# First attention: post weights applied to evicted outputs, and the inverse and the eviction ordered ahead of the next maximum and exponent

## The reference, cut to what matters

```python
logits = jnp.einsum('bhid,bhjd->bhij', q, k) * SCALE        # 4 batches, 16 heads of 8, 1024 tokens
logits = jnp.einsum('bhij,gh->bgij', logits, Wpre)          # heads mixed before the softmax
attn = jax.nn.softmax(logits, axis=-1)
attn = jnp.einsum('bhij,gh->bgij', attn, Wpost)             # heads mixed after it
out = jnp.einsum('bhij,bhjd->bhid', attn, v)
out = out.transpose(0, 2, 1, 3).reshape(b, n, DIM)
return out @ Wout.T + bout
```

## Time and profile before

| what | value |
|---|---|
| time, median of 3 runs | 2481.05 us (2480.69 to 2481.33) |
| time of the profiled execution | 2480.47 us |
| its span in the profile | 2478.7 us |
| busy in the span: PE, DVE, ACT, POOL | 89%, 84%, 74%, 50% |
| first attention in the profile | about 72 to 1506 us |
| feed-forward, second attention, feed-forward | the rest, to 2478.7 us |

### The profile page before, as it was taken

How to read it: one execution, slowest core, us unless ns; L and a number is a source line. 1 busy time by engine, 2 the same in 40 slices (tenths; PEclk the granted TensorE clock), 3 DMA queues, 4 the chain that set the end, 5 groups by cost and what they waited for, 6 DMA issues and landing times. The chain is left out here.

```text
span 2478.7 us, 62316 instructions
## 1 busy us (share of the span) xinstructions
PE 2199.3 (89%) x22576; PEld 1502.2 (61%) x22576; DVE 2077.6 (84%) x3160; ACT 1822.4 (74%) x2674; POOL 1237.8 (50%) x1482
## 2 busy tenths in 40 slices
PE   5899999999999999999999994556899999999556
PEld 3466676666766676666766664443455555555544
DVE  6899999999999999999999995655799999997473
ACT  1788888888888888888888882115799998998002
POOL 3445444444444544445444452300788888887030
PEclk9999999999999999999999997669799999999866
DMA  2799999999999999999999993006222222222001
GB/s 93 121 196 187 196 187 192 191 192 189 194 189 194 184 197 192 190 189 192 192 189 191 192 194 71 1 8 207 70 69 72 70 69 70 70 69 51 29 1 34
DMA packets 1183691, 333.54 MB, mean 135 GB/s; under 512 B 1145968, under 2 KB 1174512, under 8 KB 1183216
## 3 DMA queue, kind: packets, MB, share of 16 engines
q1 hardware_dynamic: 1182320, 326.97, 74.2%
q10 hardware_dynamic: 1152, 3.62, 0.4%
HBM read 30.57 MB, written 14.68 MB: 18 GB/s over the span
## 5 line engine op out<-in xcount | busy, mean ns | idle before, releaser
L329 PE MATMUL a_out_ps<-a_vs,a_pT 128*128 128x129 f16 x4096 | 726.0, 221 | 48.4 <-ACT a_own_out L378 46.6
L416 DVE SCALAR_TENSOR_TENSOR a_parts<-a_probs,a_parts 128x1024 f16<-128x1024 f32 x512 | 653.2, 1276 | 115.1 <-ACT a_parts L369 115.1
L333 PE MATMUL a_out_ps<-a_vs,a_pT 128*128 128x129 f16 x4096 | 724.5, 219 | 0.0
L331 PE MATMUL a_out_ps<-a_vs,a_pT 128*128 128x128 f16 x4096 | 724.4, 218 | 0.0
L361 ACT ACTIVATE a_probs<-a_score_ps,a_negmax 128x1024 f32<-128x1024 f32 x512 | 571.8, 1117 | 164.9 <-DVE a_negmax L410 164.8
L410 DVE TENSOR_REDUCE a_negmax<-a_score_ps 128x1 f32<-128x1024 f32 x512 | 621.2, 1213 | 2.4 <-PE a_score_ps L315 2.4
L369 ACT ACTIVATE a_parts<-a_probs 128x1024 f16<-128x1024 f32 x512 | 543.5, 1061 | 0.6 <-DMA a_pT<-a_parts 0.6
L329 PEld LDWEIGHTS a_out_ps<-a_vs,a_pT 128*128 128x128 f16 x4096 | 396.4, 97 | 146.1 <-ACT a_own_out L378 99.1
L331 PEld LDWEIGHTS a_out_ps<-a_vs,a_pT 128*128 128x128 f16 x4096 | 402.9, 98 | 44.6
L477 POOL TENSOR_TENSOR acc<-acc,a_own_out 128x256 f32<-128x256 f32 x256 | 247.9, 969 | 352.3 <-DVE a_parts L416 346.4
L311 PE MATMUL a_score_ps<-kh,a_qs 128*128 128x512 f16 x1024 | 388.6, 379 | 10.3 <-DVE a_qs L401 7.0
(11 more groups left out here) (199 smaller groups left out, 2701.4 us busy)
## 6 DMA issues: line engine op xcount, KB each, us to landing
a_pT<-a_parts SPq DMA_TRANSPOSE x512, 5.0
b_qs<-q_parts SPq DMA_DIRECT2D x128, 64.0 KB, 2.0
b_ks<-k_parts SPq DMA_DIRECT2D x128, 64.0 KB, 1.9
q_parts<-b_parts SPq DMA_DIRECT2D x32, 128.0 KB, 1.9
k_parts<-b_parts SPq DMA_DIRECT2D x32, 128.0 KB, 1.9
v_parts<-b_v_all SPq DMA_DIRECT2D x4, 1024.0 KB, 4.6
b_vs<-v_parts SPq DMA_DIRECT2D x32, 128.0 KB, 2.1
b_sent_pT<-b_sent_parts SPq DMA_TRANSPOSE x256, 2.3
```

Of the source, the lines that this page charges most:

```text
L329: pe.matmul(out[:, 0:D + 1], hi, vs[:, G % 2, 0, j, 0:D + 1], start=j == 0, stop=False, skip_group_check=True)
L331: pe.matmul(out[:, 0:D], hi, vs[:, G % 2, 1, j, 0:D], start=False, stop=False, skip_group_check=True)
L333: last = pe.matmul(out[:, 0:D + 1], lo, vs[:, G % 2, 0, j, 0:D + 1], start=False, stop=j == JB - 1, skip_group_check=True)
L416: dve.scalar_tensor_tensor(out=parts[:, T % RING_P, 1, :], in0=probs[:, T % RING_P, :], scalar=PSCALE, in1=parts[:, T % RING_P, 0, :], op0 ...
```

## The change

Two things change in `attend_a`.

- **Post weights.** The values are no longer scaled for each group. They are split into their 16-bit parts once a batch: `vs` has a slot for each of the four batches, the first is made ahead of the loop, the others while the batch before is worked on (steps 24, 26 and 28 of its 128). The post weights are applied to the evicted outputs by a new POOL operation `weigh(pair)` from `own_out` into `weighed`, and `add` reads `weighed`. POOL runs `weigh` of one pair and then `add` of the pair before it, and at the end one more `add`. The eviction now waits for `weigh` of the pair before last (semaphore `weighed_ready`), not for its `add`.
- **Order.** In step i of DVE the inverse now stands ahead of the maximum of tile i, in step i of ACT the eviction ahead of the exponent of tile i.

```diff
             for i in range(TILES_A + AH + 2):
+                if i >= AH + 2 and i % 2 == 0:
+                    evict((i - AH - 2) // 2)
                 if i < TILES_A:
                     exponentiate(i)
-                if i >= AH + 2 and i % 2 == 0:
-                    evict((i - AH - 2) // 2)
...
             for i in range(TILES_A + AH + 2):
+                if i >= AH + 2 and i % 2 == 0:
+                    invert((i - AH - 2) // 2)
                 if i < TILES_A:
                     row_max(i)
-                if i >= AH + 2 and i % 2 == 0:
-                    invert((i - AH - 2) // 2)
...
                 act.wait_ge(rden_ready, pair + 1)
                 if pair >= 2:
-                    act.wait_ge(added, pair - 1)
+                    act.wait_ge(weighed_ready, pair - 1)
...
-                G, t = T // TPB, T % TPB
-                if t == 0:
-                    pe.wait_ge(vlo_made, G + 1)
+                b = T // (HA * TPB)
+                if T % (HA * TPB) == 0:
+                    pe.wait_ge(vlo_made, b + 1)
...
+            def weigh(pair):
+
+                pool.wait_ge(evicted, 2 * pair + 2)
+                if pair >= 2:
+                    pool.wait_ge(added, pair - 1)
+                g = 2 * pair // TPB % HA
+                w = wpost[:, g * D:(g + 1) * D][:, None, :].broadcast_to([P, 2, D])
+                slot = 2 * pair % 4
+                pool.tensor_tensor(weighed[:, pair % 2, :, :], own_out[:, slot:slot + 2, :], w,
+                                   ALU.mult).then_inc(weighed_ready, 1)
...
             pool.memset(vs[:, :, 0, :, D:], 1.0).then_inc(ones_ready, 1)
+            high_v(0)
+            low_v(0, 0)
+            low_v(0, 1)
             pool.memset(acc[:], 0.0).then_inc(cleared, 1)
             pool.wait_ge(cleared, 1)
-            for i in range(TILES_A + AH + 4):
-                G, t = i // TPB, i % TPB
-                if i < TILES_A and t < 5:
+            for i in range(TILES_A + AH + 2):
+                b, step = i // (HA * TPB) + 1, i % (HA * TPB) - 3 * TPB
+                if b < NB and step in (0, 2, 4):
                     pace(i)
-                    if t in (0, 1):
-                        scale_v(G, t)
-                    elif t == 2:
-                        high_v(G)
+                    if step == 0:
+                        high_v(b)
                     else:
-                        low_v(G, t - 3)
-                if i >= AH + 4 and i % 2 == 1:
+                        low_v(b, step // 2 - 1)
+                if i >= AH + 3 and i % 2 == 1:
+                    pair = (i - AH - 3) // 2
                     pace(i)
-                    add((i - AH - 4) // 2)
+                    weigh(pair)
+                    if pair >= 1:
+                        add(pair - 1)
+            add(TILES_A // 2 - 1)
```

More of the change, by code:

```diff
@@ L265, in attend_a @@
         own_out = st.sb(s, "a_own_out", [P, 4, D])
+        weighed = st.sb(s, "a_weighed", [P, 2, 2, D])
         qs = st.sb(s, "a_qs", [P, 2, 2, SEQ], F16)
[L267 to L268 removed]
+        vs = st.sb(s, "a_vs", [P, NB, 2, JB, D + 2], F16)
         score_ps = [st.ps(s, f"a_score_ps{i}", [P, SEQ]) for i in range(3)]
@@ L328, in times_v @@
                     hi, lo = pT[:, T % RING_T, 0, j, :], pT[:, T % RING_T, 1, j, :]
-                    pe.matmul(out[:, 0:D + 1], hi, vs[:, G % 2, 0, j, 0:D + 1], start=j == 0, stop=False,
+                    pe.matmul(out[:, 0:D + 1], hi, vs[:, b, 0, j, 0:D + 1], start=j == 0, stop=False,
                               skip_group_check=True)
-                    pe.matmul(out[:, 0:D], hi, vs[:, G % 2, 1, j, 0:D], start=False, stop=False,
+                    pe.matmul(out[:, 0:D], hi, vs[:, b, 1, j, 0:D], start=False, stop=False,
                               skip_group_check=True)
-                    last = pe.matmul(out[:, 0:D + 1], lo, vs[:, G % 2, 0, j, 0:D + 1], start=False,
+                    last = pe.matmul(out[:, 0:D + 1], lo, vs[:, b, 0, j, 0:D + 1], start=False,
                                      stop=j == JB - 1, skip_group_check=True)
@@ L444, in pace @@
                     pool.wait_ge(lo_ready, min(i - 1, TILES_A))
-            def scale_v(G, c):
-                if c == 0 and G >= 1:
-                    pool.wait_ge(vlo_made, G)
-                own = slice(c * JB // 2, (c + 1) * JB // 2)
-                src = v[:, (G // HA) * SEQ + c * HALF:(G // HA) * SEQ + (c + 1) * HALF]
-                w = wpost[:, (G % HA) * D:(G % HA + 1) * D][:, None, :].broadcast_to([P, JB // 2, D])
-                pool.tensor_tensor(vtmp[:, own, :], src.rearrange("p (j d) -> p j d", j=JB // 2), w,
-                                   ALU.mult).then_inc(v_scaled, 1)
@@ L456, in high_v @@
-            def high_v(G):
-                pool.wait_ge(v_scaled, 2 * G + 2)
-                if G >= 2:
-                    pool.wait_ge(pv_done, TPB * (G - 1))
-                pool.tensor_scalar(vs[:, G % 2, 0, :, 0:D], vtmp[:], 1.0, 1.0, ALU.mult, ALU.mult).then_inc(vhi_made, 1)
-            def low_v(G, c):
-                pool.wait_ge(vhi_made, G + 1)
-                own = slice(c * JB // 2, (c + 1) * JB // 2)
-                last = pool.tensor_tensor(vs[:, G % 2, 1, own, 0:D], vtmp[:, own, :], vs[:, G % 2, 0, own, 0:D],
-                                          ALU.subtract)
+            def high_v(b):
+                pool.tensor_scalar(vs[:, b, 0, :, 0:D], v[:, b * SEQ:(b + 1) * SEQ].rearrange("p (j d) -> p j d", j=JB),
+                                   1.0, 1.0, ALU.mult, ALU.mult).then_inc(vhi_made, 1)
@@ L469, in low_v @@
+            def low_v(b, c):
+                pool.wait_ge(vhi_made, b + 1)
+                own = slice(c * JB // 2, (c + 1) * JB // 2)
+                src = v[:, b * SEQ + c * HALF:b * SEQ + (c + 1) * HALF]
+                last = pool.tensor_tensor(vs[:, b, 1, own, 0:D], src.rearrange("p (j d) -> p j d", j=JB // 2),
+                                          vs[:, b, 0, own, 0:D], ALU.subtract)
                 if c == 1:
                     last.then_inc(vlo_made, 1)
+            def weigh(pair):
[7 more added lines that the diff above has]
+                                   ALU.mult).then_inc(weighed_ready, 1)
@@ L472, in add @@
             def add(pair):
-                pool.wait_ge(evicted, 2 * pair + 2)
+                pool.wait_ge(weighed_ready, pair + 1)
                 at = (2 * pair // TPB // HA) * TPB + 2 * pair % TPB
-                slot = 2 * pair % 4
-                pool.tensor_tensor(acc[:, at:at + 2, :], acc[:, at:at + 2, :], own_out[:, slot:slot + 2, :],
+                pool.tensor_tensor(acc[:, at:at + 2, :], acc[:, at:at + 2, :], weighed[:, pair % 2, :, :],
                                    ALU.add).then_inc(added, 1)
```

4 lines of the change are left out of this document (1 added, 3 removed).

## The result

The changed kernel takes 2459.04 us (2456.97 to 2459.72) against 2481.16 us: a ratio of 0.991, 95% interval 0.9893 to 0.9927, so 22 us won where 57 were forecast. Its profiled execution took 2459.72 us with a span of 2457.9 us.

A forecast was written before the change was run, and what follows sets the result against it. DVE and ACT were taken to set the pace while PE waits 0.87 us a group. Gains of 53.9 (62 groups), 1.3 and 3.5 less 1.9 give 56.8 us: 2424 us, range 2418 to 2450.

The forecast's parts named there:

- What bounds the kernel now: First attention: a DVE-ACT loop, 5.00 us for two tiles, makes the eviction late; PE loses 0.87 us a group of 22.15.
- The eviction leaves the path and fits into ACT's wait; DVE's inverse costs nothing: New order: loop falls from 5.00 to 4.51 us; eviction of 0.49 to 0.62 us fits ACT's 0.63 us wait; inverse free.
- POOL's wait of 0.4 us is inside the 0.87: Eviction's wait for POOL's `add`, 0.4 us on the loop's third pair, goes; already counted in PE's 0.87 us a group.
- Low part behind `weigh` and `add`, up to 0.33 us: DVE's low part overlaps POOL's two operations by at most 0.33 us, taken as lost four times a group: 1.3 us.
- The start: POOL's new work at the very start may hold the first `low_q`: 0 to 1.1 us lost, 0.5 taken.
- The end: After the last eviction POOL does more, +1.4 us; DVE is no longer late, 3.5 us less.
- The pace after it: DVE 19.75, ACT 18.8, loop 19.2 to 20.3 us a group, all under PE's 21.28, so PE takes over; 0.87 won.
- The prediction's own signs of being wrong: Low parts of 1.6 us or more; L369 waiting for `a_pT`; PE stalled at L311; turns above 2.66 us at clock 1.00.
- Another pace than PE's takes hold: Rival: DVE or transpose landings set the pace, only part of the gain, 2453 or 2456 us; chance 0.15.
- It does nothing: Rival: PE's stall is a late transpose, or the transpose queue takes no more than one in 2.77 us; 2481 us, chance 0.04.

The follow-up runs named there:

- e10: Changed kernel with two stages ahead of 64 transposes each, free of engine waits, the second beside 3200 PE matmuls; 2810.05 us with both stages.
- e7: Changed kernel with 32 more long-fulfilled waits in each POOL step, packed into 16 more instructions; 2470.82 us, ratio 0.9952 to the kernel before.
- e6: Changed kernel with the high part's two products in one 256-column matmul, 44 instead of 60 PE instructions a tile; 2431.76 us, ratio 0.9796.
- e5: Changed kernel with two transposes a tile, the high part's sent as soon as it is made; 2573.69 us, ratio 1.0373 to the kernel before.
- e12: Changed kernel with one 128x4096 transpose for two tiles and eight instead of four slots for the parts; 2427.58 us, ratio 0.9789.
- e3: Changed kernel with five instead of four slots for the parts; 2460.62 us, ratio 0.9916 to the kernel before.
- e4: Changed kernel with only the high part transposed and read twice by the product, half the transposed data; 2423.65 us, ratio 0.9764.
- e11: Changed kernel with the old order of inverse and eviction, weights on the outputs, only the high part transposed; 2454.07 us, ratio 0.9893.
- e1: Kernel before with the new order of inverse and eviction alone, post weights still folded into the values; 2548.94 us, ratio 1.0271.
- e9: Kernel before with the new order alone and eight instead of four slots for the evicted outputs; 2459.29 us, ratio 0.9910.

## Why the prediction was wrong

**The queue's time adds up.** With 2.473 us a transpose, 0.86 us a 16 KB fetch (both e10) and 0.17 us an 8 KB one (e7, the least certain of the three), the queue is taken, out of 1200 us, for:

| kernel | transposes | q8 | q14 | us taken |
|---|---|---|---|---|
| before | 434 | 102 | 46 | 1169 |
| after | 443 | 105 | 44 | 1193 |
| e6 | 451 | 79 | 46 | 1191 |
| e7 | 439 | 104 | 98 | 1192 |
| PE's pace, after's fetches | 451 | 105 | 44 | 1213 |

Before, the queue was 97% full with DVE and ACT setting the pace; the change moves it to 99.4%, and there it stops. PE's pace would need 1213 us of every 1200. For e7 this isn't a test of its own, since its count gave the 0.17. Halves in e5 come to (1200 - 97 x 0.86 - 45 x 0.17) / 817 = 1.36 us each, so a whole, which is 2.47, saves 0.24 us over two halves. A pair in one transpose would by that be 4.70 us, with the fetches 2.57 us a tile, under 2.66; e12 bears out that it is under 2.66. (The expectation had 4.47 us, with the fetches not yet taken out of the halves.)

The packet records give a count that needs none of these prices: the time, out of the same 1200 us, in which no packet of a transpose is under way. It is 33 us before, 12 after, 15 in e3, 9 in e6, 16 in e7 and 1 in e5, against 499 in e4. So by this count too the queue is 97% full before the change and 99% after it. In e12 it is 31 us at PE's pace: (1200 - 31) / 451 = 2.59 us a tile, fetches included, is about what the paired transposes need.

**By the prediction's steps.** *What bounds the kernel now*: right; the loop of DVE and ACT gave way, and where the queue has room (e4) exactly 2.66 us comes out. *The eviction leaves the path and fits into ACT's wait; DVE's inverse costs nothing*: right by e4 and e11, 30 us. *POOL's wait of 0.4 us is inside the 0.87*: right, since 0.48 is left of the stall in e11, but its weight was underrated. In the new order that wait would have grown to 229 us (e1). So the weights' move is what lets the order pay, or else more slots (e9). *Low part behind `weigh` and `add`, up to 0.33 us*: 1.45 instead of 1.21 us, thus 0.24, in two of four pairs (at 688.26 and 700.18 us). The overlap was 0.37 us, a little over the 0.33 of the working, and it cost nothing in e4. The Trainium skill ("SBUF — State Buffer", section "Who interferes with whom") has the overlap go to whoever started first, and this low part began 0.37 us before the `add` at 687.90 ended:

```profile
687.90 0.73 POOL L476 TENSOR_TENSOR acc<-acc,a_weighed 128x256 f32<-128x256 f32 x1
```

The trace agrees on who yields: the `add` kept its 0.73 us, and the low part lost 0.24 us of the 0.37. *The start*: forecast 0.5 us lost, measured 0.2 won.

*The end*: forecast 2.1 us shorter, measured 4.8 longer. The queue was behind when the last scores came: SP issued the last transpose at 1473.43 us, 4.1 us after the last low part had ended, against 2.7 us before. In e4, without that, the end is 2.7 shorter.

**The step that failed** is "The pace after it", which compares DVE, ACT and the loop with PE's 21.28 us and then says "so PE takes over". The queue of transposes is missing from that list; at 8 x 2.719 = 21.75 us a group it takes over instead. The change won 22 of the 57 us, and e12, which gives the queue room, 31 more. The prediction's own signs of being wrong came: waits of L369 for `a_pT`, and turns above 2.66 us in a granted clock of 1.00. The rival "Another pace than PE's takes hold" named the wait (the landing of T-4) and it named 2453 us, from half of each stall, and 2456 us, from an eviction that doesn't fit into ACT's wait. That they lie near 2459 us is luck: the eviction fits (e4), and nothing halves the stall. It set 7.9 us of room against at most 7.2 us "from issue". A full queue delays the issue itself, and that time isn't in a figure counted from issue. The rival "It does nothing" did ask whether the queue takes one in 2.77 us, and put this aside because nobody waited for DMA. But a queue that is 97% full makes no one wait yet, and shows only what happens to be under its limit. The figure that put it out, the 261 GB/s of the Trainium skill ("DMA: Bandwidth & Descriptors", section "Latency and other measured facts"), was as little use. The skill gives it for transposes with a non-contiguous middle dimension and more for contiguous ones; here 0.52 MB in 2.473 us is 212 GB/s (e10), with the queue free of everything else.

**What stays open.** After's queue turns over at 2.719 us against 2.473 + 0.86 / 4.2 + 0.02 = 2.70 us by the parts; 0.02 us a tile isn't explained by them. It is about the size of the 12 us in which the queue stood empty (0.027 us a tile); what left it empty then wasn't followed. The 2.2 us behind the stage weren't followed either. The 0.86 us rest on the one run of e10. Why a fetch stops the transposes for over 1 us was not tried. Nor was it separated what behind SP sets the 2.47 us of a transpose; SP's own work on an issue isn't it, as the 1.32 us after an idle stretch show.

## What to carry to other kernels

Before an engine is named as the next bound, put every queue beside it as a rate: transfers times the time of one in a full queue, plus what interrupts it, against the pace that is hoped for. Latency from issue and the absence of waits say nothing of a queue that is 97% full; the issue's own duration does, against that of an issue after an idle stretch (2.45 and 1.32 us here). If its rate is the limit, another buffer gives nothing (e3), while fewer and larger transfers do (e12, 31 us more). And two edits that each remove a stall may each be worth the whole gain.

## What the hardware showed beyond that

- PE's instruction fetches, 16 KB each and one in 4.2 tiles, cost PE nothing and the running transposes 0.86 us each, 7.5% of the time of this stage's queue (105 x 0.86 of 1200 us is 90 us). Fewer instructions on a full engine can thus speed up a DMA queue (e6).
- A transpose of 128x2048 two-byte elements takes 2.47 us alone, 212 GB/s. Cut in two it is 2 x 1.36 = 2.7 us (e5, fetches taken out); joined with its neighbour it is about 2.59 us a tile with the fetches in it (e12), where the changed kernel's needs (1200 - 12) / 443 = 2.68.
- POOL's 8 KB fetches cost about 0.17 us each (0.07 to 0.27), by one run with 60 more of them; for half the bytes of PE's that is at most a third of the price.
